# GPS graph network on one core: layer 1's neighbour sum in destination order, with accumulating scatters

## The reference

```python
xn = layernorm(x)
x = x + gnn0(xn, src, dst) + linear_attention0(xn)      # gnn0: edge softmax, summed over each dst
x = x + ffn0(layernorm(x))                              # top-k routed
xn = layernorm(x)
support = xn @ W                                        # layer 1, the sum that the change is about
gathered = support[dst] * edge_weight[:, None]
x = x + segment_sum(gathered, src, 6250) + b + linear_attention1(xn)
x = x + ffn1(x)                                         # experts, layernorm
```

## Time and profile before

| | us |
|---|---|
| median of 3 runs | 7841.31 (7838.94 to 7847.16) |
| span of the profiled execution | 7837.5 |
| PE busy in it | 4906.9 (63%) |
| DVE busy | 3746.0 (48%) |
| POOL busy | 4885.1 (62%) |
| ACT busy | 1981.3 (25%) |

### The profile page before, as it was taken

One profiled execution on the slowest core, in us unless ns is written; L12 is line 12 of the kernel. 1 busy time (PEld: TensorE's weight loads), 2 busy tenths in 40 slices (PEclk: granted clock), 3 DMA queues, 4 the chain that ended last, 5 costly groups with the idle time before them and its releaser, 6 DMA issues. The chain is left out here.

```text
span 7837.5 us, 121180 instructions
## 1 busy us (share of the span) xinstructions
PE 4906.9 (63%) x21606; PEld 3530.6 (45%) x21607; DVE 3746.0 (48%) x11942; ACT 1981.3 (25%) x4749; POOL 4885.1 (62%) x5920
## 2 busy tenths in 40 slices
PE   0365354889999999619834549235555555665692
PEld 0133342556666666418712438224444443444582
DVE  7896526666677777631121330353333333333314
ACT  0221152445555555305322213000000000001351
POOL 0002767777777777667747767777777777773002
PEclk9987676999999999859967879678877878778796
DMA  2100002444444444200010000023333333331000
GB/s 83 47 0 10 4 7 66 116 116 116 116 116 116 116 116 116 67 15 3 3 37 3 6 12 3 3 74 105 106 106 106 105 106 106 106 106 51 12 0 34
DMA packets 542397, 496.32 MB, mean 63 GB/s; under 512 B 411923, under 2 KB 438923, under 8 KB 541579
## 3 DMA queue, kind: packets, MB, share of 16 engines
q0 software_dynamic: 200192, 432.72, 20.1%
q1 hardware_dynamic: 215435, 57.63, 3.4%
q10 hardware_dynamic: 126720, 5.46, 1.1%
HBM read 465.14 MB, written 30.23 MB: 63 GB/s over the span
## 5 line engine op out<-in xcount | busy, mean ns | idle before, releaser
L999 POOL DMA_INDIRECT XN<-table,XN x3128 | 2986.9, 955 | 832.0 <-issue 705.5
L425 POOL DMA_INDIRECT records<-slot_rec,slot_pos x1564 | 1545.3, 988 | 457.1 <-issue 456.8
L1313 PE MATMUL gcn_psE<-XN,gcn_pE 128*125 x3520 | 1164.7, 491 | 1035.8 <-SPq L979 1026.2
L1313 PEld LDWEIGHTS gcn_psE<-XN,gcn_pE 128*125 128x125 f32 x3520 | 816.3, 242 | 1384.1 <-issue 1233.4
L1133 PE MATMUL gat_psE<-XN,gat_pE 128*125 x3520 | 882.2, 394 | 3.4 <-ACT gat_pE L1186 2.9
L1341 DVE TENSOR_TENSOR room<-room,gcn_psE 125x256 f32 x440 | 185.3, 421 | 1193.5 <-PE gcn_psE L1313 1192.7
L73 POOL TENSOR_TENSOR cell<-cell 1x1 int32<-1x1 int32 x1006 | 189.9, 189 | 856.1 <-DMA slot_pos<-spill_pos 808.3
L1133 PEld LDWEIGHTS gat_psE<-XN,gat_pE 128*125 128x125 f32 x3520 | 638.1, 191 | 85.8 <-issue 4.6
L541 ACT ACTIVATE gcn_w_stage<-room 125x512 f32 (+1 forms) x25 | 15.6, 622 | 2083.3 <-PEq L115 2083.3
L1329 DVE TENSOR_SCALAR gcn_pE<-iota_n,gcn_lk,gcn_rec 128x125 f32<-128x125 f32 x1760 | 505.4, 359 | 16.0
L478 POOL TENSOR_TENSOR X<-X,room x150 | 124.8, 866 | 607.8 <-DVE room L520 604.6
(11 more groups left out here) (358 smaller groups left out, 7678.9 us busy)
## 6 DMA issues: line engine op xcount, KB each, us to landing
XN<-table,XN POOLq DMA_INDIRECT x3128, 2.8
records<-slot_rec,slot_pos POOLq DMA_INDIRECT x1564, 2.1
XN<-records SPq DMA_DIRECT2D x782, 6.0 KB
table<-XN SPq DMA_DIRECT2D x10, 1250.0 KB
gat_rec<-records ACTq DMA_DIRECT2D x440, 6.0 KB
gcn_rec<-records ACTq DMA_DIRECT2D x440, 6.0 KB
X<-in_x SPq DMA_DIRECT2D x1, 6250.0 KB
out_x<-X SPq DMA_DIRECT2D x5, 1250.0 KB
```

Source lines behind the costliest of these rows:

```text
L425: pool.indirect_dma_start(out=rec_d[self.which], out_offset=bass.IndirectOffsetOnAxis(ap=slot_pos[:, h, j:j + 1], axis=0), in_=slot_rec[:, ...
L999: pool.indirect_dma_start(out=rows_t[:, s, j, :], out_offset=None, in_=table, in_offset=bass.IndirectOffsetOnAxis(ap=rec_g[:, s, j, 1:2].b ...
L1313: last = pe.matmul(psE[d][0:B, 0:D], pE[:, d, j, :], rows_t[:, slot_of(g), j, :].rearrange("p a w -> p (a w)"), start=(j == 0), stop=(j == ...
```

## The change

Layer 1's sum is done in `dst` order, with the records as they lie. A tile is 128 records; NT = 1564 tiles and 50 blocks give TS = 1613 steps (tile, block), taken four at a time as NQ = 404 quads. In `push_rows`, per quad:

- SP reads the four block numbers into registers and loads four tiles of records (1.5 KB each).
- DVE copies the four `src` columns as floats (`places`), builds four weighted one-hots [128 x 125] (`hots`), compares each tile's `src` with all `src` of the tile (`same`), and finds which records have a later one with the same `src` in the tile (`targets`: a product and a sum over [128 x 512], three small operations); those are sent to rows from 6250 on, which nobody reads. The others go to their `src` row.
- PE transposes the four `src` columns (`sources`), multiplies one-hot by equality matrix (`mixes`), which sums equal `src` of a tile, and multiplies the result with the block's 125 rows of `XN`, straight from SBUF (`messages`). So rows are no longer gathered.
- ACT copies one [125 x 512] and two [128 x 512] results out of PSUM.
- POOL issues four indirect DMAs, each of which adds 128 rows of 1 KB to its own copy `acc[j]` of the sum in DRAM (`compute_op=ALU.add`). Ahead of each it waits for the one before to the same copy and runs `settle`.

The copies are set to zero in the sort stage by four DMAs of 6.55 MB each, ahead of the loading of `X`, which has moved there from the second sort. `collect_rows` loads the four copies and adds them up on DVE. The second `sort_edges`, `Places` in `sums0`, all record moves beside other stages, `table1` with its stores, and `edge_sums` with the zeroing of `U` are gone. `edge_softmax` and the arithmetic of all other stages stay as they were.

```diff
+NT = EP // P
+TS = NT + NB - 1
+QUAD = 4
+NQ = -(-TS // QUAD)
+TP = NQ * QUAD
+COPIES = 4
+NACC = 6400
...
-    table1 = nc.dram_tensor("table1", [N, D], F32).ap()
+    acc = [nc.dram_tensor(f"acc{i}", [NACC, D], F32).ap() for i in range(COPIES)]
...
+                        sp.dma_start(after_[0:P - 1, :], key[1:P, 0:2]).then_inc(loaded, 16)
+                        sp.wait_ge(zero_set, 1)
+                        for dst in acc:
+                            sp.dma_start(dst.rearrange("(p r) d -> p r d", p=P),
+                                         zeros[:, :].unsqueeze(1).broadcast_to([P, NACC // P, D])).then_inc(cleared, 16)
                         sp.wait_ge(rec_done, 1)
+                        sp.dma_start(spill_rec, rec[:, :, :]).then_inc(spilled, 16)
+                        sp.dma_start(rec_d.rearrange("(p t) w -> p t w", p=P), rec[:, :, :]).then_inc(spilled, 16)
+                        sp.dma_start(X[:, :, :], rows(A["x"])).then_inc(x_in, 16)
+                        sp.wait_ge(x_in, 16)
+                        sp.wait_ge(tiles_set, 1)
+                        sp.dma_start(tile_blk_d, tile_blk[:, :]).then_inc(spilled, 16)
+                        sp.dma_start(tile_blkf_d, tile_blkf[:, :]).then_inc(spilled, 16)
+                        sp.wait_ge(spilled, 64)
+                        sp.wait_ge(cleared, 16 * COPIES)
...
-                mv = mover(name, turns)
-                        mv.sp(sp)
-                        mv.pool(pool)
...
-                            if edge:
-                                places.blocks(k * 2, 2)
...
+        def push_rows():
...
+            RG = 4
...
+                rows_t = words[:, 0:RG * QUAD * D].rearrange("p (r s d) -> p r s d", r=RG, s=QUAD)
...
+                src_done, same_mm, eq_done, hot_done, idx_done, a_mm, a_done, m_mm, m_done, own, settled = (
...
                 with nc.Block() as block:
                     @block.sync
                     def _(sp):
+                        def body(t, s):
+                            if not early(t, s, RG):
+                                sp.wait_ge(hot_done, t * RG + s - RG + 1)
+                            for j in range(QUAD):
...
+                                    b = sp.value_load(tile_blk[0:1, bass.ds(x, 1)], min_val=0, max_val=NB - 1)
...
+                                sp.dma_start(rec_t[:, s, j, :], rec_v[bass.ds(tile, 1), :, :].rearrange("t p w -> (t p) w")).then_inc(rec_ready[s], 16)
...
+                    @block.tensor
+                    def _(pe):
+                        def sources(t, s):
+                            k, d = t * RG + s, s % 2
+                            pe.wait_ge(src_done, k + 1)
+                            if not early(t, s, 2):
+                                pe.wait_ge(eq_done, k - 1)
+                            for j in range(QUAD):
+                                last = pe.transpose(psS[d][:, j * P:(j + 1) * P], srcf[:, d, j:j + 1].broadcast_to([P, P]), ident[:, :])
+                            last.then_inc(same_mm, 1)
+                        def mixes(t, s):
+                            k, d = t * RG + s, s % 2
+                            pe.wait_ge(hot_done, k + 1)
+                            pe.wait_ge(eq_done, k + 1)
+                            if not early(t, s, 2):
+                                pe.wait_ge(a_done, k - 1)
+                            for j in range(QUAD):
+                                last = pe.matmul(psA[d][0:B, j * P:(j + 1) * P], hot[:, d, j, :], eq[:, d, j, :], start=True, stop=True)
+                            last.then_inc(a_mm, 1)
+                        def messages(t, s):
+                            k, d = t * RG + s, s % 2
+                            pe.wait_ge(a_done, k + 1)
+                            if not early(t, s, 2):
+                                pe.wait_ge(m_done, k - 1)
+                            for j in range(QUAD):
+                                b = pe.value_load(tile_blk[0:1, bass.ds(k * QUAD + j, 1)], min_val=0, max_val=NB - 1)
+                                last = pe.matmul(psM[d][j // 2][:, (j % 2) * D:(j % 2 + 1) * D], mix[:, d, j * P:(j + 1) * P],
+                                                 one(XN[0:B, bass.ds(b, 1), :]), start=True, stop=True)
+                            last.then_inc(m_mm, 1)
+                        def body(t, s):
+                            if at(t, s, 1):
+                                sources(*at(t, s, 1))
+                            mixes(t, s)
+                            if at(t, s, -1):
+                                messages(*at(t, s, -1))
...
                     @block.scalar
                     def _(act):
+                        def take_mix(t, s):
+                            k, d = t * RG + s, s % 2
+                            act.wait_ge(a_mm, k + 1)
+                            if not early(t, s, 2):
+                                act.wait_ge(m_mm, k - 1)
+                            act.activation(mix[:, d, :], psA[d][0:B, :], ACT.Copy).then_inc(a_done, 1)
+                        def take_rows(t, s):
+                            k, d = t * RG + s, s % 2
+                            act.wait_ge(m_mm, k + 1)
+                            if not early(t, s, RG):
+                                for j in range(COPIES):
+                                    act.wait_ge(added_rows[j], (k - RG + 1) * 16)
+                            for h in range(2):
+                                last = act.activation(rows_t[:, s, 2 * h:2 * h + 2, :].rearrange("p s d -> p (s d)"), psM[d][h][:, :], ACT.Copy)
+                            last.then_inc(m_done, 1)
+                        def body(t, s):
+                            take_mix(t, s)
+                            if at(t, s, -1):
+                                take_rows(*at(t, s, -1))
...
                     @block.vector
                     def _(dve):
                         st = Steps(dve, own)
+                        dve.wait_ge(tables_in, 32)
+                        def places(t, s):
+                            k, d = t * RG + s, s % 2
+                            dve.wait_ge(rec_ready[s], t * (16 * QUAD) + 16 * QUAD)
+                            if not early(t, s, 2):
+                                dve.wait_ge(same_mm, k - 1)
+                                dve.wait_ge(idx_done, k - 1)
+                                dve.wait_ge(hot_done, k - 1)
+                            dve.tensor_copy(srcf[:, d, :], rec_t[:, s, :, 1].bitcast(I32)).then_inc(src_done, 1)
+                            st.mark(dve.scalar_tensor_tensor(lk[:, d, :], tile_blkf[:, bass.ds(k * QUAD, QUAD)], -float(B), rec_t[:, s, :, 0],
+                                                             ALU.mult, ALU.add))
+                        def hots(t, s):
+                            k, d = t * RG + s, s % 2
+                            if not early(t, s, 2):
+                                dve.wait_ge(a_mm, k - 1)
+                            for j in range(QUAD):
+                                last = dve.tensor_scalar(hot[:, d, j, :], iota_n[:, :], lk[:, d, j:j + 1], rec_t[:, s, j, 2:3],
                                                          ALU.is_equal, ALU.mult)
+                            last.then_inc(hot_done, 1)
+                        def same(t, s):
+                            k, d = t * RG + s, s % 2
+                            dve.wait_ge(same_mm, k + 1)
+                            if not early(t, s, 2):
+                                dve.wait_ge(a_mm, k - 1)
+                            dve.wait_ge(src_done, k + 1)
+                            st.mark(dve.tensor_scalar(far[:, d, :], srcf[:, d, :], -1.0, trash[:, 0:1], ALU.mult, ALU.add))
+                            dve.tensor_tensor(eq[:, d, :, :], psS[d][:, :].rearrange("p (s n) -> p s n", s=QUAD),
+                                              srcf[:, d, :].unsqueeze(2).broadcast_to([P, QUAD, P]), ALU.is_equal).then_inc(eq_done, 1)
+                        def targets(t, s):
+                            k, d = t * RG + s, s % 2
+                            dve.wait_ge(eq_done, k + 1)
+                            st(dve.tensor_tensor(later[:, :, :], eq[:, d, :, :], lower[:, :].unsqueeze(1).broadcast_to([P, QUAD, P]), ALU.mult))
+                            st(dve.tensor_reduce(cnt[:, :], later[:, :, :], AX.X, ALU.add))
+                            st(dve.scalar_tensor_tensor(cnt[:, :], cnt[:, :], 0.0, far[:, d, :], ALU.is_gt, ALU.mult))
+                            if not early(t, s, RG):
+                                for j in range(COPIES):
+                                    dve.wait_ge(added_rows[j], (k - RG + 1) * 16)
+                            dve.tensor_tensor(idx[:, s, :], cnt[:, :], srcf[:, d, :], ALU.add).then_inc(idx_done, 1)
                         def body(t, s):
+                            same(t, s)
+                            if at(t, s, 1):
+                                places(*at(t, s, 1))
```

(57 more changed lines are left out.)

407 lines of the change are left out of this document (185 added, 222 removed).

## The result

The kernel before took 7840.12 us (median of 4 runs, 7838.11 to 7847.16), the changed one 8239.62 (4 runs, 8233.05 to 8264.51): ratio 1.0515, 95% interval 1.05 to 1.0531. The forecast was 7439, faster. The time lies in the range and close to the first rival at 1.5 times (8126).

A forecast was written before the change was run, and what follows sets the result against it. No engine bounds the whole; each stage has its own bound, `edge_sums` POOL's issue rate. 7837.5 - 777.7 - 2000.5 + 15 + 80 + 2281 (`push_rows`, POOL-paced) = 7435, with 3.8 for the median 7439 us; range 7290 to 8500.

The forecast's parts named there:

- the first rival: `push_rows`: describing an addition takes POOL longer; at 1.5 times 7.3 us a quad, total 8126; at twice 8926; chance 0.25.
- the bounding of the scatter's issue: `push_rows`: POOL's issue of an accumulating scatter put between 0.95 and 1.98 us, value taken near the low end.
- Interference: `push_rows`: 0.28 us a quad added to POOL's 5.32 for DVE operations hitting scatters and for what adding costs the issue.
- the port rule: `push_rows`: DVE's two-port mode stops POOL writing descriptors; 8.1 us a quad, total 8449; chance 0.03.
- Landing: `push_rows`: at most 4.9 us, covered by the 5.6 between scatters to one copy; as rival, total 8611, chance 0.12.
- DVE next in line: `push_rows`: DVE close behind POOL at 4.7 to 5.25 us a quad; as pace-setter 6.25, total 7702, chance 0.10.
- What goes: Removed work: 777.7 us from second sort, stage ends, `ln_c`, zeroing of `U` and `sums0`, plus 2000.5 of `edge_sums`.
- the stage ends: Ends of 12 stages where only POOL moves records: 486.8 us together, 475 to go after allowance for barriers.
- The first sort: Sort stage gains zeroing of the copies and the load of `X`: ends near 152 us instead of 139, taken as +15.
- `collect_rows`: Stage that loads and adds the copies: 70 us at the 16-engine rate and 10 for the last slice, +80.
- Break-even: `push_rows`: with all else as forecast, the change gains nothing at 6.6 us a quad, 1.65 a scatter.
- the slower cases: `push_rows`: longer description of additions (0.25), landing as the chain (0.12) and the port rule (0.03), together 0.40.

The follow-up runs named there:

- half the width: Changed kernel with accumulating scatters of 512-byte rows instead of 1 KB, and `collect_rows` loaded over 128 partitions; 9198.17 us, one run on a slower chip.
- the first profile: Profiled execution of the changed kernel as it is, the longest of its four runs; 8264.51 us, span 8262.8.
- Whole slices: Changed kernel with each `collect_rows` slice loaded by one DMA into 128 partitions instead of 112 and 13; 8191.89 us against 8233.11.

## Why the prediction was wrong

*The step that failed.* It is the bounding of the scatter's issue. The prediction put both ends rightly (0.95 and 1.98) and then chose a value near the low one, "since gather and scatter, 1 KB and 12 bytes, all take 0.94 to 0.99: size and direction don't matter". That sentence is true, and half the width shows it again. But those rows vary size and direction only; the change varied the operation, and no row of before bore on it. The value is 1.564, above the point of 1.31 from which the first rival decides. 1616 x (1.873 - 1.40) = 764 of the 770 us missing are this (1.873 is (7455.3 - 4430.9) / 1615 of the first profile); the rest is the chain's fill, 25 us instead of 15, less a shorter end.

*The rival that came true* was priced by its mechanism, an issue 1.5 times as long: 7.3 a quad, total 8126. It is 1.57 times and 7.5 a quad. That it is near the rival's number at 1.5 times is no proof of the rival's mechanism. Its reason, more descriptors on the read side, isn't shown: the packets above the rest go up fourfold at 128 rows and not at all at 16, and the additional time is mostly the same in both. The Trainium skill, "Collectives: The Full Stack", section "The bandwidth ceiling", has a reducing DMA emit two read descriptors per chunk; twice the description would have been 1.98, the trace has 1.564, and its packets don't show a doubling at any number of rows. The chance of 0.25 was too low for a cost that no row excluded and on which the sign hung.

*Interference* (part of the 0.28 a quad) isn't there. With writes the quad is 5.48 and not 5.6. The 0.16 above 5.32 is in the issue itself: 0.993 us, with the gap of 0.37 of the earlier trace rows, are 1.36, and the 1.33 was read behind a scatter of 0.96. The median of the issue is 5 ns above its minimum, with DVE's product with `lower` run once in every quad. The 15.91 us of the earlier trace rows came beside 50 such operations in a row, and nothing like that runs in `push_rows`. The same holds for the port rule that the prediction weighed ("SBUF — State Buffer", section "SBUF: two separate sides", of the Trainium skill): it would have given 8.1 a quad with plain scatters, and these took 5.48 with all four `hots` in the quad. The prediction took the rule wider than it stands there, since `targets`' sum has one input and is no copy; with the `hots` alone it would be 5.32 + 1.44 = 6.8, and the trace doesn't show that either. Whether the `hots` ran in the two-port mode, no view shows.

*Landing*: forecast under 4.9 and hidden; it is 3.8, hidden. *DVE next in line*: forecast 4.7 to 5.25 a quad. With writes of 64 rows the scatters are 1.26 us apart where nothing stops them (the median from start to start), 5.04 a quad, and the quads come (6534.6 - 4397.7) / 404 = 5.29 apart; with 16 rows they need 1.20, 4.8 a quad, and come (6427.8 - 4394.0) / 404 = 5.03 apart. So the other engines begin to show between 5.0 and 5.3, which is where the forecast had DVE; which of them it is wasn't measured by itself.

*What goes* was right in each term: the second sort to 0.4 us, `edge_sums` to 1, `sums0` to 4.5 (259.5 instead of 263, at a clock of 0.96), and the stage ends to 25, which is what the clock in `att1` took. The first sort too: its end was put near 152 and is at 152.2.

*`collect_rows`* was 39 us too cheap. The 16-engine rate was scaled up from the load of `X`, which supposes that the 16 engines are used evenly and as well. (The rows allow a lower figure too: 114 GB/s at a share of 32.7% are 349 GB/s at a full share.) Whole slices do reach that rate (386 GB/s in their steady part, 375 were forecast, and the stage takes the 80 us that were forecast); the split into 112 and 13 partitions doesn't. The step overlooked the shape of the transfer.

*Break-even* was given as 6.6 us a quad, 1.65 a scatter. The quads took (3051.5 - 19) / 404 = 7.51. Above the break-even that is 3051.5 - 2281 - 402 = 368 us, and 39 for `collect_rows` make 407, where 399.5 lie between the medians. The sum was right around its one unknown number, and it had said that everything hung on it.

*The chances* don't add up as told: 0.40 for the slower cases less 0.03 is 0.37 and not 0.39, which leaves 0.60 for faster. It changes nothing in the judgement.

## What to carry to other kernels

Where the sign of a change hangs on one unknown price, and no row varies what the change varies, the choice between the bounds isn't evidence: rows that agree with each other in size and direction say nothing on another operation. Give such a price half the chance on either side, and measure it alone before anything is built on it; one kernel with the scatters as they are and one with writes would have settled this in two runs. In these runs an indirect DMA that adds costs POOL 0.57 us more to issue than one that writes, mostly per DMA and not per row, and 1616 of them in a stage that POOL paces made 811 us. Halving the rows of each hardly helps; by the same numbers what would help is fewer of them, which wasn't tried.

## What the runs showed of the hardware

- An indirect DMA of 128 rows from SBUF to DRAM takes POOL 0.993 us to issue when it writes, 1.564 when it adds; with 16 rows 0.843 and 1.282. Adding rows of 512 bytes takes what adding rows of 1 KB takes (1.563 and 1.564). With one scatter in flight the issue is the same (1.562).
- From issue to landing an addition of 128 rows of 1 KB takes 3.8 us (median, one in flight), a write 2.4 (median, with four copies). Additions that follow one another on one tensor, each after the landing of the last, come 4.5 to 4.6 us apart.
- Above 16 packets that each scatter has, a writing scatter has a packet for four rows at 128 rows and at 64 and one for each row at 16; an adding one has a packet for each row at all three.
- Some 26 MB in 1 KB pieces load at 217 GB/s through DMAs of 112 and of 13 partitions, and at 327 through DMAs of 128 partitions, over the whole stage; the busy share of the DMA engines is over 90% in both.
